# Reordering the steps of a fused first pass: input statistics a row ahead, and a new order of small work on VectorE and ScalarE

## The reference, cut to what matters

```python
x = x + 0.5 * ffn(layernorm(x), W_ffn, bias)       # ternary weights
x = x + mamba(layernorm(x), ...)
x = x + 0.5 * ffn(layernorm(x), W_ffn, bias)
# mamba:
u, z = split(x @ W_in.T)
u = silu(conv4(u) + conv_b)                        # causal, 4 taps, per channel
dt_r, Bm, Cm = split(u @ W_xproj.T)                # 64 + 16 + 16
dt = softplus(dt_r @ W_dt.T + b_dt)
h[t] = exp(dt * A) * h[t-1] + dt * Bm * u          # 16 states a channel
y = (sum_n h * Cm + u * Dskip) * silu(z)
out = y @ W_out.T
```

## Time and profile before

| | us |
|---|---|
| median of 3 runs | 2809.26 |
| lowest, highest | 2805.38, 2812.28 |
| profiled execution | 2817.4 |
| its span, first to last instruction | 2815.3 |
| PE, DVE, ACT, POOL busy in it | 2398.9, 2382.5, 2037.6, 1838.2 |

### The profile page before, as it was taken

How to read it: one execution, slowest core, us unless ns; L and a number is a source line. 1 busy time by engine, 2 the same in 40 slices (tenths; PEclk the granted TensorE clock), 3 DMA queues, 4 the chain that set the end, 5 groups by cost and what they waited for, 6 DMA issues and landing times.

```text
span 2815.3 us, 37729 instructions
## 1 busy us (share of the span) xinstructions
PE 2398.9 (85%) x12448; PEld 1378.9 (49%) x12448; DVE 2382.5 (85%) x3197; ACT 2037.6 (72%) x3769; POOL 1838.2 (65%) x1449
## 2 busy tenths in 40 slices
PE   3599899899898736799899899998998898898898
PEld 1244444444443325555555555555555555555553
DVE  6676766766765769999999999999999999999992
ACT  3336666765766757888888888888888888888883
POOL 1112222322221149999999999999999999999981
PEclk8799999999998867899999999999999999999999
DMA  7753242323233267676776676676676776667754
GB/s 245 245 202 134 91 136 98 128 98 136 88 130 113 87 225 183 148 168 148 168 167 157 156 181 149 161 179 149 158 181 146 166 165 162 162 151 171 164 104 96
DMA packets 200289, 429.25 MB, mean 152 GB/s; under 512 B 44512, under 2 KB 93920, under 8 KB 199840
## 3 DMA queue, kind: packets, MB, share of 16 engines
q1 hardware_dynamic: 160928, 284.23, 30.5%
q0 software_dynamic: 39168, 142.62, 27.3%
HBM read 190.86 MB, written 110.10 MB: 107 GB/s over the span
## 4 chain that ended last, share of the span: by engine, by line
DVE 32%; PE 15%; POOL 10%; issue 6%; ACT 1%; POOLq 0%; DVEq 0%; ACTq 0%
DVE h L1446 20%; DVE y L1459 7%; POOL dbu L1229 7%; PE p_g L1584 7%; PE p_ht L1550 5%; PE p_g L1593 2%; DVE x L1493 1%; POOL y L1248 1%; DVE q L1472 1%; DVE x L1483 1%; PE p_g L1574 1%; DVE small L57 1%; POOL y L1263 0%; POOL dbu L1234 0%; ACT p_da L1318 0%
## 5 line engine op out<-in xcount | busy, mean ns | idle before, releaser
L1446 DVE TENSOR_TENSOR_SCAN h<-p_da,dbu 128x512 f32<-128x512 f32 x1024 | 1187.6, 1207 | 24.3 <-ACT p_da L1318 16.5
L1229 POOL TENSOR_TENSOR dbu<-shared,bb 128x1024 f32<-128x1024 f32 x352 | 894.8, 2616 | 13.9 <-DVE h L1446 13.0
L1318 ACT ACTIVATE p_da<-shared,neg_a 128x255 f32<-128x255 f32 x1408 | 605.1, 467 | 171.4 <-DVE h L1446 167.2
L1550 PE MATMUL p_ht<-ident,h 128*128 128x128 f32 x4096 | 562.7, 296 | 133.7 <-DVE h L1446 132.9
L1550 PEld LDWEIGHTS p_ht<-ident,h 128*128 128x128 f32 x4096 | 511.4, 154 | 210.9 <-DVE h L1446 185.9
L1229 POOL TENSOR_TENSOR dbu<-dtu,bb 128x1024 f32<-128x1024 f32 x160 | 419.1, 2620 | 7.2 <-DVE h L1446 7.2
L1459 DVE SCALAR_TENSOR_TENSOR y<-p_ht,ct,y 128x1024 f32<-128x1024 f32 x272 | 345.2, 1269 | 21.9 <-PE p_ht L1550 21.6
L1584 PE MATMUL p_g<-wo,tokt 128*128 128x512 f16 x1536 | 354.0, 388 | 3.2 <-ACT tokt L1361 2.1
L1593 PE MATMUL p_g<-wz,xz 128*128 128x512 f16 x1536 | 344.5, 381 | 0.0
L1318 ACT ACTIVATE p_da<-dt,neg_a 128x255 f32<-128x255 f32 x640 | 274.9, 467 | 77.8 <-DVE h L1446 76.3
L436 POOL TENSOR_TENSOR late<-dt,u 128x512 f32<-128x512 f32 x64 | 83.1, 1298 | 371.5 <-DVE dt L696 371.5
(11 more groups left out here) (143 smaller groups left out, 3123.1 us busy)
## 6 DMA issues: line engine op xcount, KB each, us to landing
y<-y_part POOLq DMA_DIRECT2D x224, 512.0 KB, 5.7
bb<-b_scratch SPq DMA_DIRECT2D x128, 256.0 KB, 4.4
xin<-in_x SPq DMA_DIRECT2D x32, 512.0 KB, 5.2
x_scratch<-x SPq DMA_DIRECT2D x32, 512.0 KB, 4.8
y_scratch<-late SPq DMA_DIRECT2D x32, 512.0 KB, 5.4
dt_scratch<-dt SPq DMA_DIRECT2D x64, 256.0 KB, 2.1
dtu_scratch<-late SPq DMA_DIRECT2D x64, 256.0 KB, 2.4
y<-y_scratch SPq DMA_DIRECT2D x32, 512.0 KB, 5.2
```

Source lines behind the costliest of these rows:

```text
L1229: nc.gpsimd.tensor_tensor(state[:, 4 * f:4 * f + 4, :], dtu[k % 3], bb[n // NB % 2][:, n % NB:n % NB + 1, :].to_broadcast([P, G // 2, T2]) ...
L1318: ins_ = nc.scalar.activation(p_da[p % 2][:, k * T2 + 1:(k + 1) * T2], dt[m % NR][:, k, 1:], ACT.Exp, scale=neg_a[:, g, n:n + 1])
L1446: nc.vector.tensor_tensor_scan(h[n % 2][:, 2 * p:2 * p + 2, :].rearrange("p g t -> p (g t)"), p_da[p % 2][:], dbu[n % 2][:, 2 * p:2 * p + ...
L1550: mm = nc.tensor.transpose(p_ht[t][:, g * P:(g + 1) * P], h[n % 2][:, g, t * P:(t + 1) * P], ident[:])
```

## The change

For rows 8 on the input row is loaded at the head of SP's step, ahead of its stores; its statistics are taken by VectorE two rows ahead, after phase 0, instead of one row ahead at the head of the step; GpSimd scales them after the second normalisation's. Steps with i <= 0, and the one with (i, j) = (1, 0), keep the old place (the latter does both). VectorE takes the low half of row k + 1 ahead of phase 1's units. ScalarE does silu of group 2j - 1 ahead of phase 0, and the d units of phases 2 and 3 as a pair: Relu and Abs of each, then Exp of each, then Ln of each. In row j = 3 the units per phase go from 1, 2, 1, 1 to 1, 1, 2, 1, so that d6 and d7 are such a pair, as are d1 and d2 in row j = 1.

```diff
@@ -179,7 +179,7 @@
 
         units = [("y", 0), ("x", 0), ("y", 1), ("c", 0), ("d", 0), ("y", 2), ("d", 1), ("y", 3), ("d", 2), ("d", 3),
                  ("y", 4), ("d", 4), ("y", 5), ("d", 5), ("y", 6), ("d", 6), ("d", 7), ("y", 7)]
-        per_phase = [(1, 1, 1, 1), (1, 1, 1, 2), (1, 1, 1, 1), (1, 2, 1, 1)]
+        per_phase = [(1, 1, 1, 1), (1, 1, 1, 2), (1, 1, 1, 1), (1, 1, 2, 1)]
         NU = len(units) // 2
 
         def last(k):
@@ -207,6 +207,10 @@
             if isinstance(k, int):
                 return 0 < k <= L // P
             return f_on
+
+        def stats_late(i, j):
+
+            return i <= 0 or (i, j) == (1, 0)
 
         def had_u(i, j):
 
@@ -380,11 +384,11 @@
 
                 def step(i, par, j, f_on, u_on, s_on):
                     k = (i + 1) * TT1 + j
+                    if not last(k + 1):
+                        load_x(k + 2, j % 2, k * P + 2 * P)
                     if s_on:
                         s_stores(i - 1, j, 0)
                         s_stores(i - 1, j, 1)
-                    if i <= 0:
-                        load_x(k + 2, j % 2, k * P + 2 * P)
                     w_transfers(w_first(i, j))
                     if j == 0 and turned(k, f_on):
                         store_xz(i, par)
@@ -394,8 +398,6 @@
                     if f_on:
                         wait_alone(sp, x1_done, k * 2 + 2)
                         sp.dma_start(dram["x1"][bass.ds(k * P, P), :], x1[j % 2][:]).then_inc(x1_stored[j % 2], 16)
-                        if i > 0 and not last(k + 1):
-                            load_x(k + 2, j % 2, k * P + 2 * P)
                     w_transfers(w_second(i, j))
                     if s_on:
                         s_stores(i - 1, j, 2)
@@ -454,12 +456,14 @@
                         if isinstance(k, int) and k == 0:
                             pool.wait_ge(const_done, 1)
                         nc.gpsimd.tensor_tensor(x1[j % 2][:], xin[j % 2][:], half_bias[:], ALU.add).then_inc(xb_done, 1)
-                        if not last(k):
+                        if stats_late(i, j):
                             row_scale(pool, nc, vn[0], minus_half, sn[0], stats_ready[0], pow_done[0],
                                       scale_ready[0], xn_done[0], k + 1)
-                    if f_on:
                         row_scale(pool, nc, vn[1], minus_half, sn[1], stats_ready[1], pow_done[1],
                                   scale_ready[1], xn_done[1], k)
+                        if i > 0 and not last(k + 1):
+                            row_scale(pool, nc, vn[0], minus_half, sn[0], stats_ready[0], pow_done[0],
+                                      scale_ready[0], xn_done[0], k + 2)
                     for t, m, q, split in w_items(i, j):
                         if t % 8 == 3:
                             over_partitions(m, RABSMAX)
@@ -500,6 +504,15 @@
                 def s_work(d, j, phase):
                     for unit in s_units(j, phase, "xd"):
                         s_unit(d, *unit)
+
+                def s_last(d, j):
+                    pair = s_units(j, 2, "d") + s_units(j, 3, "d")
+                    for v, _, g in pair:
+                        relu_abs(d, v, g)
+                    for v, _, g in pair:
+                        softplus_exp(d, v, g)
+                    for _, _, g in pair:
+                        softplus_ln(d, g)
 
                 def s_unit(d, v, kind, g):
                         if kind == "x":
@@ -603,10 +616,10 @@
                         u_work(*before)
                     if f_on and not last(k):
                         normalise(0, xin[(j + 1) % 2][:], k + 1)
+                    if had_u(i, j):
+                        silu(before[0], par if j else 1 - par, before[1])
                     if s_on:
                         s_work(i - 1, j, 0)
-                    if had_u(i, j):
-                        silu(before[0], par if j else 1 - par, before[1])
                     w_high(w_first(i, j))
                     if f_on:
                         normalise(1, x1[j % 2][:], k)
@@ -622,8 +635,7 @@
                     if u_on:
                         silu(i, par, 2 * j)
                     if s_on:
-                        s_work(i - 1, j, 2)
-                        s_work(i - 1, j, 3)
+                        s_last(i - 1, j)
                     if i == 0 and j == TT1 - 1:
                         nc.scalar.activation(neg_a[:], neg_a[:], ACT.Exp).then_inc(a_done, 1)
                         act.wait_ge(a_done, 1)
@@ -795,7 +807,7 @@
                         for b in range(2):
                             hi, lo = (into[:, a, jj // 2, 4 * b:4 * b + 4, (jj % 2) * P:(jj % 2 + 1) * P] for a in range(2))
                             low(1, k - 1, hi, lo, b)
-                    if f_on and not last(k):
+                    if f_on and stats_late(i, j):
                         wait(dve, x_loaded[(j + 1) % 2], (f * 2 + (j + 1) // 2 + 1) * 16)
                         row_stats(dve, nc, xin[(j + 1) % 2], stats[0], mv[0], vn[0], small[:, 40:41], ln_chain[0],
                                   stats_ready[0], scale_ready[0], k + 1)
@@ -816,13 +828,17 @@
                                   scale_ready[1], k)
                     if s_on:
                         s_work(d, 1 - par, j, 0)
+                    if i > 0 and not last(k + 1):
+                        wait(dve, x_loaded[j % 2], (f * 2 + j // 2 + 2) * 16)
+                        row_stats(dve, nc, xin[j % 2], stats[0], mv[0], vn[0], small[:, 40:41], ln_chain[0],
+                                  stats_ready[0], scale_ready[0], k + 2)
                     if u_on:
                         conv(i, 2 * j)
-                    if s_on:
-                        s_work(d, 1 - par, j, 1)
                     if f_on and not last(k):
                         for b in range(2):
                             low(0, k + 1, xt[:, 0, 4 * b:4 * b + 4, :], xt[:, 1, 4 * b:4 * b + 4, :], b)
+                    if s_on:
+                        s_work(d, 1 - par, j, 1)
                     w_work(w_second(i, j))
                     if s_on:
                         s_work(d, 1 - par, j, 2)
```

## The result

The changed kernel took 2818.19 us in the median of 15 runs (2810.63 to 2823.22), the kernel before 2809.02 (2805.38 to 2817.90) beside it: ratio 1.0028, 95% interval 1.0019 to 1.0036. The forecast was 2762, range 2735 to 2793. A gain of 47 us was forecast and a loss of 9 came. The profiled execution took 2818.87 us, its span is 2816.9.

A forecast was written before the change was run, and what follows sets the result against it. TensorE, idling behind late VectorE, was taken to set the 110.80 us block; 96.81 + 2.5 waits + 2.5 low clock + 0.8 hand-overs = 102.6, saving 8.2. Six blocks: 49, net 47.5, so 2762 us, range 2735 to 2793.

The forecast's parts named there:

- ScalarE's wait for the scale goes, the input row is early, 18 table loads a block: Before ScalarE's first normalisation: 8.77 us and VectorE's 3.94 us load wait go; table loads fall from 21 to 18.
- j=0: "low half 11.6 ... against 27.2: no wait": Row j=0: VectorE's low halves end at 11.6 and 25.1 us, against TensorE's 27.2, so TensorE does not wait.
- My list: The prediction's row-by-row schedule of TensorE, VectorE and ScalarE from trace durations; its waits sum to 2.5 us a block.
- low clock: TensorE's 1.2 GHz level after idle bits: 2.5 us a block forecast, for two waits left; before 5.17 us.
- VectorE's durations, taken from the earlier trace: VectorE's schedule: low half 1.25, convolution 2.8, sum 1.4, statistics 1.75, y unit 0.6, d unit 2.6 us.
- The slower rival: VectorE stands in mid-row for the late input load; at 12 us landing 53 lost, 2862 us; chance 0.05.
- j=2: y5 waits 1.5: End of row j=2: TensorE waits 1.5 us for y5's bank, which VectorE's y4 frees at 23.3; before 2.18 + 2.62.
- Hand-overs: Handing over between engines, not in the list: put at 0.8 us a block, bounds 0 and 4.
- end of the loop: Last rows after the loop start with more owed: 1.6 us lost, net saving 47.5.
- The pair is off the path except for ending 2.6 us sooner: ScalarE's paired d units: 3.9 us less table loads a block, off the path except the row's end, 2.6 us earlier.
- the lateness only moves: Late y and d units stop TensorE at small units' banks; 10 of the 14 us return, 2787 us; chance 0.16.

The follow-up runs named there:

- both causes away: Changed kernel, bias sum cut to one column from row 8 on, second normalisation's high and low half ahead of d6 and d7's softplus: 2764.92 us.
- the two good parts: Kernel before with only load, statistics and scale a row ahead and silu ahead of softplus: 2779.53 us, ratio 0.9887.
- after_bias_early: Changed kernel, with GpSimd's bias sum of row k + 1 right after the second scale of row k: 2809.02 us, ratio 0.9988.
- only_ahead: Kernel before with only the input load, statistics and scale a row ahead: 2790.09 us, ratio 0.9920.
- after_onecol: Changed kernel with the bias sum of rows 8 on cut to one of 1024 columns: 2790.72 us, ratio 0.9935.

## Why the prediction was wrong, step by step

- *ScalarE's wait for the scale goes, the input row is early, 18 table loads a block.* Right. ScalarE's wait for the scale is 17.2 us over 248 to 881 us, VectorE no longer waits for the row, and the block has 6 Exp, 6 Ln and 6 silu loads. The part alone is worth 22 us.
- *j=0: "low half 11.6 ... against 27.2: no wait".* This step failed. My list had the second normalisation's low half done at 11.6 us and the u product from 8.45 on, and it set only the row's last step (25.1) against the end of the row (27.2), not this low half against its reader. TensorE's code has the wait ahead of the u product of j=0: all four rows of a stretch must be split. Even with my own durations it is a wait of 3.1 us plus low clock; measured, 4.77 plus 2.66. Of the 1.6 us beyond the list, 0.95 is GpSimd's product on the d unit (0.69 to 1.64).
- *VectorE's durations, taken from the earlier trace rows.* This failed too. They were read in a row where no GpSimd operation held them. The change moved GpSimd's sum onto the first tap (0.55 to 2.53), and products onto the middle taps and the d unit (about 1 us each). The trace before had the sign: its first tap has a mean of 601 ns in the earlier trace rows against 0.55 us in the timeline above it, since six of the 46 began beside a sum, five near its end (0.65 to 0.67 us) and one, at 860.03, 0.11 us after its start (2.53 us). Cutting the sum alone gave 27 us. The slower rival asked about GpSimd's sum only as the thing that the load waits for, and looked at landing times; they fell, from 5.2 us in the median to 3.3, and it was not what happened.
- *j=2: y5 waits 1.5.* The mechanism was right, the size wrong: 4.95, and 2.96 without the sum. Of the 3.45 us too much, 1.98 is the sum on the first tap (2.53 at 505.67), 1.02 the product on the middle taps (2.56 at 518.66), and 0.45 is left over.
- *Hand-overs, low clock, end of the loop.* For the block about right together: with both causes away it is 102.0, forecast 102.6, by terms that offset each other: its waits are 4.2 and not 2.5, its low clock 1.7 and not 2.5, its hand-overs nothing. The end of the loop was too small, 1.6 us against 3.5 in the changed kernel and 5.2 with both causes away.
- *The pair is off the path except for ending 2.6 us sooner.* Wrong in j=3. There VectorE gets d6 and d7 in a bunch, later, ahead of the low half that a u product wants. The pair costs 14 us alone and 31 on top of the two good parts.
- *The rival "the lateness only moves"* is nearest to what happened; I gave it 0.16 and let it return 10 of 14 us. All 14 came back: 112.24 us a block against 110.80.

## What to carry to other kernels

When work is moved, list for each of its products every reader and the time at which the first of them wants it, and check the new list against all of them, not against the end of the row. Durations of one engine taken from a trace hold beside what its neighbour did at that moment: look what GpSimd runs while a VectorE row is short, and where both will run after the change. Here waits at a row's end that named an evacuation were the debt of an engine that was 70 to 80% busy, and putting one evacuation first shifted the wait to the next reader.

## What the runs showed of the hardware

Some of VectorE's operations on SBUF end only behind a GpSimd tensor operation that began before them: a first tap of 0.55 us took 2.53, an addition of two tiles 0.69 took 1.64 and 2.81, each ending 0.3 to 0.6 us behind GpSimd's. Even a copy of three columns, 0.16 us, took 1.64 beside the moved sum (`after_bias_early`, 531.50). Others are not held: in the kernel before, input statistics at 337.89 took their usual 0.68 us with 1.94 us of the sum still to run, and in `after_bias_early` no y evacuation (one input in the bank) took more than 0.69 us, though GpSimd had up to 1.09 us to run. So the length of a GpSimd operation matters by what VectorE does beside it. Scans were not looked at for it.

A 512 KB load landed in 3.3 us in the median in the changed kernel and in 3.6 in `only_ahead`, instead of 5.2 before. In `after_onecol`, with the load in the same place of SP's order, it was 4.3, so what sets it is not separated.

One TensorE wait of 3.11 us was followed by 2.1 us of extra FFN time and 0.9 us of extra transposes at the lower clock, as much as before after two waits of 4.8 together. The price varies from block to block: after the same wait in the next block (3.27 us) it was 1.3 and 0.55.
